# Layer 2 of the experts three parts behind layer 1, with the third norm and the residual one part later

## The reference

```
x = x + layernorm(attn(layernorm(x)))        # attn: gate g = sigmoid(x Wg + bg), h = scan of (1-g) h + g x, h Wo + bo
x = x + layernorm(ffn(layernorm(x)))

def ffn(xf):                                 # N = 16384 rows of D = 256
    eid   = argmax(softmax(xf @ router_w + router_b))
    rank  = place of the row among those of its expert;  valid = rank < C        # C = 320
    buf[eid, rank] = xf where valid          # E = 8 experts of C rows
    h     = relu(buf @ w1[e] + b1[e])        # layer 1 of each expert: 256 -> H = 1024
    y     = h @ w2[e] + b2[e]                # layer 2 of each expert: 1024 -> 256
    yov   = relu(xf @ ow1 + ob1) @ ow2 + ob2 # overflow network
    return y[eid, rank] where valid, else yov
```

## Time and profile before

| | us |
|---|---|
| median of 3 runs | 1139.61 (1139.54 to 1140.75) |
| the profiled execution's own time | 1139.46 |
| its span in the profile | 1137.5 |
| TensorE busy | 1118.9 (98%) |
| VectorE busy | 989.5 (87%) |
| ScalarE busy | 772.7 (68%) |
| GpSimd busy | 661.6 (58%) |

### The profile page before, as it was taken

The page is one execution under the profiler, slowest core; times in us unless marked ns, Lnnn a source line. Parts: engine busy times, 40 slices in busy tenths (PEclk is TensorE's granted clock), DMA queues, the critical chain, the costliest instruction groups (busy, mean ns, idle before and its releaser), DMA issues. The chain is left out here.

```text
span 1137.5 us, 24653 instructions
## 1 busy us (share of the span) xinstructions
PE 1118.9 (98%) x7341; PEld 996.5 (88%) x7341; DVE 989.5 (87%) x2795; ACT 772.7 (68%) x1433; POOL 661.6 (58%) x734
## 2 busy tenths in 40 slices
PE   8999999999999999999999999999999999999996
PEld 4788988888888898888888888898889988899996
DVE  6888899899999999998989898999999888688885
ACT  5366676667766667666677666677666776687882
POOL 3556666656666665666666666566666655324443
PEclk9999999999999999999999999999999999999998
DMA  8211043222222222222222222222222220435430
GB/s 259 68 48 57 20 126 80 72 76 56 74 74 74 74 74 73 69 72 70 72 53 72 73 57 72 60 71 74 74 74 74 55 93 20 128 126 175 159 126 31
DMA packets 186314, 92.46 MB, mean 81 GB/s; under 512 B 121403, under 2 KB 182509, under 8 KB 186148
## 3 DMA queue, kind: packets, MB, share of 16 engines
q1 hardware_dynamic: 179108, 86.65, 27.3%
q0 software_dynamic: 7168, 5.34, 1.6%
HBM read 53.82 MB, written 38.76 MB: 81 GB/s over the span
## 5 line engine op out<-in xcount | busy, mean ns | idle before, releaser
L691 ACT ACTIVATE hid<-psH,biasT 128x512 f32<-128x512 f32 (+1 forms) x312 | 202.7, 650 | 206.0 <-PE psH L1432 203.9
L1538 PE MATMUL psY<-W_hi,hid_hi 128*128 128x256 f32 x1168 | 336.1, 288 | 0.3 <-DVE hid_lo L1112 0.2
L1541 PE MATMUL psY<-W_hi,hid_lo 128*128 128x256 f32 x1168 | 330.5, 283 | 0.0
L1540 PE MATMUL psY<-W_lo,hid_hi 128*128 128x256 f32 x1168 | 330.3, 283 | 0.0
L1430 PE MATMUL psH<-xfT_hi,W_hi 128*128 128x512 f32 (+1 forms) x624 | 235.8, 378 | 0.3 <-ACT hid L691 0.2
L1112 DVE TENSOR_TENSOR hid_lo<-hid,hid_hi 128x512 fp32r<-128x512 f32 (+1 forms) x308 | 200.1, 661 | 40.3 <-ACT hid_hi L696 37.0
L1431 PE MATMUL psH<-xfT_lo,W_hi 128*128 128x512 f32 (+1 forms) x624 | 235.0, 377 | 0.0
L1432 PE MATMUL psH<-xfT_hi,W_lo 128*128 128x512 f32 (+1 forms) x624 | 232.6, 373 | 0.0
L1538 PEld LDWEIGHTS psY<-W_hi,hid_hi 128*128 128x128 f32 x1168 | 223.0, 191 | 9.2 <-issue 1.5
L1540 PEld LDWEIGHTS psY<-W_lo,hid_hi 128*128 128x128 f32 x1168 | 223.3, 191 | 6.0
L1541 PEld LDWEIGHTS psY<-W_hi,hid_lo 128*128 128x128 f32 x1168 | 223.1, 191 | 0.0
(11 more groups left out here) (179 smaller groups left out, 2167.5 us busy)
## 6 DMA issues: line engine op xcount, KB each, us to landing
xin<-L_attn_x SPq DMA_DIRECT2D x32, 512.0 KB, 3.5
stage<-L_ffn_w SPq DMA_DIRECT2D x16, 1024.0 KB, 5.5
out<-outt SPq DMA_DIRECT2D x31, 512.0 KB, 2.8
stage<-L_attn_x SPq DMA_DIRECT2D x26, 512.0 KB, 3.5
stage<-tok SPq DMA_DIRECT2D x416, 32.0 KB
xbuf<-zrow SPq DMA_DIRECT2D x1, 2590.0 KB, 16.8
xin<-xbuf SPq DMA_DIRECT2D x8, 259.0 KB, 5.3
stage<-L_ffn_ow SPq DMA_DIRECT2D x2, 1024.0 KB, 8.8
```

The lines of the kernel that those rows point to most:

```text
L691: act.activation(hid[j % 2][:, at:n], psH[:, j % 2, at:n], ACT.Relu, bias=bias).then_inc(s_hid, 1)
L1538: pe.matmul(dst, hi, w[0][:, j, :], start=(j == 0 and (tail or t % 2 == 0)), stop=False, skip_group_check=True)
L1540: pe.matmul(dst, hi, w[1][:, j, :], start=False, stop=False, skip_group_check=True)
L1541: last = pe.matmul(dst, lo_, w[0][:, j, :], start=False, stop=(j == HC - 1), skip_group_check=True)
```

## The change

Three places move. TensorE's loop runs B(j-3) behind A(j) instead of B(j-2), by the new constant LAG = 3 (`if j >= LAG`, `layer2(now, j - LAG, ...)`); the waits that stood ahead of B(0) move with it. ScalarE runs `norm3` behind part 4's copy, not part 3's. VectorE runs the residual in part 5, not part 4, except in the last expert. One line is added at the top of the file, so all line numbers are one higher after.

```
--- before.py
+++ after.py
@@ -26,6 +26,7 @@
 QUAD = P // TG
 SQ = 32
 PIPED = 6
+LAG = 3
 SHARED2 = 31
 EPS = 1e-5
 NOWHERE = 1.0e6
@@ -908,7 +909,7 @@
                     if not more and j == 0:
                         act.wait_ge(s_l2, cnt(now, HC, 0) + EL1)
                     relu(now, j, C, biasT[:, bass.ds(col, 1)], EL1, tail=not more)
-                    if j == 3 and more:
+                    if j == 4 and more:
                         if live(prev, E):
                             norm3(prev, ET, NG)
                         else:
@@ -1380,7 +1381,7 @@
                             moments(3, last_group, TG)
                     if j == 3 and not live(nxt, E):
                         rows3(prev, ET)
-                    if j == 4:
+                    if j == (5 if live(nxt, E) else 4):
                         if live(prev, E):
                             residual3(prev)
                         else:
@@ -1731,16 +1732,16 @@
                             last = layer2(now, j, t + 1, W2[u], EL1, t0=t, tail=True)
                         last.then_inc(s_l2, 1)
                     return
-                for j in range(HC + 2):
+                for j in range(HC + LAG):
                     if j < HC:
                         layer1(now, j, C, W1[u], EL1)
                     if j == HC - 1 and live(nxt, E):
                         transposes1(nxt, ET, NG)
-                    if j >= 2:
-                        if j == 2:
+                    if j >= LAG:
+                        if j == LAG:
                             pe.wait_ge(s_y, cnt(now, 2, 0) + 2 * NG)
                             pe.wait_ge(s_we_lo, cnt(now, 8, 8))
-                        layer2(now, j - 2, ET, W2[u], EL1)
+                        layer2(now, j - LAG, ET, W2[u], EL1)
 
             for u in range(2):
                 estep(0, u)
```

## The result

| | before | after |
|---|---|---|
| median of the runs, us | 1139.68 (22 runs) | 1141.30 (22 runs) |
| ratio, 95% interval | | 1.0015 (1.0008 to 1.0021) |
| span of the profiled execution, us | 1137.5 | 1139.4 |

The changed kernel is 1.6 us slower, 0.15%. Forecast were 1141.0 us and +1.4.

What follows compares the result with a forecast made beforehand. TensorE's instruction stream was taken to set the time (busy 1118.9 of 1137.5 us). Steady experts +2.1 and expert 0 -0.7 gave +1.4 on 1139.46: 1140.9, or 1141.0 as median; range 1139.3 to 1142.7.

Steps and rivals of the forecast that it cites:

- (1): TensorE, experts 1 to 6: A(3) waits for the ReLU of part 1, 0.355 us lost per expert, +2.1 us.
- (2): ScalarE: third norm behind part 4's copy delays the ReLU of part 5; A(7) has 0.65 us slack, price 0.
- (3): VectorE: residual one part later, stretched hid_lo becomes part 6's; B(6) has 0.9 us slack, price 0.
- (4): End of an expert: four B, not three, ahead of the next A(0); longer cover worth nothing.
- (5): Expert 0: A(6) no longer waits behind the norm; next A(0) 0.71 us earlier, taken as -0.7.
- Rival (a): Expert 0 gives nothing back, 1141.7 us; if the norm also delays A(7) in every expert, 1143.8; chance 0.23.
- Rival (b): A(3) in steady experts: no pause seen, total -2.6 us, 1137.0; chance 0.07.
- (c): A(3): loss smaller, pipeline refills without 0.10 more; +0.8 us, 1140.4; chance 0.2 with its like.

Runs made afterwards that it cites:

- four halves: Changed kernel with layer 1 of experts 0 to 6 writing to two halves each of psH and psA: 1136.9 us; layer 2 two parts behind: 1142.4 us.
- its two shifted forms: Four halves with layer 2 two parts behind, plus 16 semaphore increments ahead of TensorE's or ScalarE's first wait: 1141.9 and 1141.8 us.
- its shifted form: Changed kernel plus 16 semaphore increments ahead of TensorE's first wait: 1141.3 us.

## Why the prediction was right, point by point

The forecast was +1.4 us, and +1.6 was measured, inside the range and in the narrower one that had a chance of 0.5.

(1) A(3)'s pause, the term that decides: 0.36 and 0.35 us an expert forecast in experts 2 and 6, from the end of the ReLU of part 1 plus 0.05 plus 0.10. The pause, its releaser, the 0.05 and the 0.10 all stand in the rows after, in each of experts 0 to 6, and the run that brings that ReLU forward removes them. The size was a little low: 0.39 an expert, 2.35 in all instead of 2.1. The difference is the first ReLU, 0.02 to 0.09 us later against A(0) in experts 2 to 6 than before, which I took as unchanged; with the residual back, where it is unchanged, the pace is 17.00, +0.34. One reading of the rows before was loose: B(0) came 0.15 after the end of its hid_lo, not 0.05 as A(2) after its ReLU, so that wait may not be all of its pause. The sum does not use it, since it goes from start to start.

(2) The norm: hidden, as forecast. A(7)'s slack was put at 0.65 us and is 0.73 (ReLU of part 5 done at 1037.74, A(7) at 1038.47). That the norm's move has to come with the distance I did not say in the prediction; the two runs that differ in it alone show what it carries: 4.6 us of the total (1145.7 and 1141.1).

(3) The residual: hidden, with 0.9 us of slack at B(6), as forecast, and 1141.1 against 1141.3 without its move. The stretched hid_lo moved from part 5 to part 6 and takes 1.12 us, as before; it ends 0.34 us after the end of GpSimd's copy (1040.93). The W_lo ahead of it is not stretched (0.68 us). This agrees with the rule of the Trainium skill (SBUF — State Buffer, "Who interferes with whom") that a VectorE instruction with two SBUF inputs contends with a GpSimd instruction that reads SBUF, and that the one issued second is the one that waits.

(4) The longer cover at the end of an expert: worth nothing, as forecast.

(5) Expert 0: -0.71 forecast, -0.69 measured. The slacks held by little: A(7) starts at 1004.47 and its ReLU is done at 1004.23; hid_lo of part 6 is done at 1006.91 + 1.12 = 1008.03, for B(6) at about 1008.16.

Rival (a), an expert 0 that gives nothing back or a norm that reaches A(7), did not come. Rival (b), no pause at A(3), is refuted by the row that names its releaser; (c), a reload cheaper than 0.10, by the row after it (0.25 us from the first matmul to the second). The sum 2.35 - 0.69 = 1.66 agrees with the medians' 1.62. Among the chances, 0.19 for slower and 0.76 for same should by their own parts be 0.18 and 0.77.

One part of the good fit is luck. The late take-over of psY in experts 2 to 6 was nowhere in the prediction. Here it cost 0.05 us an expert at most; in the kernel with four halves and two parts of distance, where the first ReLU is late too, holding the loads shows such lateness to be worth 3.3 us. Nothing in the prediction would have told the two cases apart.

What the prediction did not say is when a third part of distance would pay. With two halves it costs 0.40 us an expert (16.65 to 17.05, one edit apart; 0.35 against the run with the residual back, where nothing is late). With four halves it saves 0.29 (16.63 to 16.34; the 16.63 is that of the kernel with the loads held, which keeps the lateness out of it, so these two differ in the loads as well). And at two parts of distance four halves are worth nothing by themselves (16.65 and 16.63): each pays only with the other.

## What to carry to other kernels

When a consumer stage is moved one step further behind its producer, count the buffers between the producer and what drains it first. Here psH has two halves, so the producer's fourth block ran into the drain of its second, and the wait changed its place from B(0) to A(3) and grew; with four halves the same distance paid. And where the drain is late, look at what stands between two of its instructions on their engine: one weights piece of 0.6 us, moved by one part, was worth 3.5 us.

## What the runs showed of the hardware

In the waits that the rows show clearly, a TensorE block starts 0.04 to 0.06 us after the end of the instruction it waited for (A(2), A(3), A(6) after a ReLU; B(6) of expert 0 after a hid_lo that ends at 1007.88, with four halves). Its second matmul comes 0.25 us after the first instead of 0.147 (320 columns), or 0.22 instead of 0.12 (256 columns): such a wait costs 0.10 us more than itself.

VectorE and ScalarE, which both wait for TensorE at the start of experts 2 to 6, began 0.5 to 1.5 us late in some orders. In the four-halves kernel at two parts of distance and its two shifted forms VectorE's take-over of psY came 0.7 to 1.8 us after A(0) instead of 0.2 to 0.4, and ScalarE's first ReLU 1.6 to 2.0 instead of 1.1 to 1.3. In the changed kernel, its shifted form and that with ScalarE unrolled only the take-over was late (1.0 to 1.4); the first ReLU stayed within 0.15 us of its place. In all six SyncE issued the load of W2 and GpSimd its last scatter within 0.1 us of each other, from 0.6 us ahead of A(0) to 0.05 behind it; holding either back ended the lateness in the one kernel where it was tried, and with the loads held the total fell by 3.3 us (1142.4 to 1139.1). Three kernels without any lateness had the two just as close to each other, from 0.12 us ahead of A(0) to 0.24 behind it, so this is a part of the condition at best.
